# Value products in one group, and a new order of side tiles, turns and vector steps

## The reference

```
x = x + 0.5 * ffn(layernorm(x))      # "1"
x = x +       attn(layernorm(x))     # "2"
x = x + 0.5 * ffn(layernorm(x))      # "3"

ffn(x):  h = relu(x @ W_fc.T)**2;  y = h @ W_proj.T      # 128 -> 512 -> 128
         mem = 0; 5 times: reset = mem > 1; mem = 0.9*mem + y - reset; count += (mem > 1)
         return count / 5
attn(x): q, k, v = split(x @ w_qkv); per head h:
         p = softmax(q k^T / 8 - slope_h * |i - j|, masked above the diagonal)
         return concat(p v) @ w_out + b_out
```

## Time and profile before

| | |
|---|---|
| median of the runs | 1765.89 us |
| profiled execution, span | 1764.1 us |
| TensorE products busy | 1676.8 us, 95% |
| VectorE busy | 1206.1 us, 68% |
| ScalarE busy | 1289.0 us, 73% |
| POOL busy | 920.2 us, 52% |
| 16 DMA engines busy, queue q1 | 42.9% |
| value products (L388) | 2048 instructions, 361.0 us busy |
| transposes of turns (L373) | 2560 instructions, 373.6 us busy |

### The profile page before, as it was taken

One profiled execution on the slowest core, in us unless ns is written; L12 is line 12 of the kernel. 1 busy time (PEld: TensorE's weight loads), 2 busy tenths in 40 slices (PEclk: granted clock), 3 DMA queues, 4 the chain that ended last, 5 costly groups with the idle time before them and its releaser, 6 DMA issues.

```text
span 1764.1 us, 39796 instructions
## 1 busy us (share of the span) xinstructions
PE 1676.8 (95%) x10902; PEld 1259.1 (71%) x10902; DVE 1206.1 (68%) x4272; ACT 1289.0 (73%) x3446; POOL 920.2 (52%) x1258
## 2 busy tenths in 40 slices
PE   4899999999999999999999999999999999999996
PEld 3767777677776777767777676776777677677775
DVE  6575776748777585775858768586785848767563
ACT  2687876777877787876877768687777868868781
POOL 2455554555545455545555545465454545546451
PEclk8999999999999999999999999999999999999998
DMA  2555453435434435443545434444443544434430
GB/s 73 114 109 111 85 119 75 102 82 109 101 81 107 89 84 108 92 104 76 105 93 107 96 82 107 90 87 107 90 103 78 109 95 94 102 82 101 94 82 13
DMA packets 80562, 164.80 MB, mean 93 GB/s; under 512 B 12880, under 2 KB 30928, under 8 KB 80208
## 3 DMA queue, kind: packets, MB, share of 16 engines
q1 hardware_dynamic: 80336, 162.12, 42.9%
HBM read 6.88 MB, written 4.19 MB: 6 GB/s over the span
## 4 chain that ended last, share of the span: by engine, by line
PE 69%; DVE 19%; issue 8%; POOL 2%; ACT 1%; DVEq 1%; DMA 1%; SPq 0%; POOLq 0%; ACTq 0%
PE bank L388 12%; PE bank L373 12%; PE bank L343 7%; PE bank L359 7%; PE bank L431 7%; PE bank L360 6%; PE bank L439 6%; PE bank L345 5%; PE bank L344 5%; DVE spikes L615 3%; DVE negsc L558 3%; DVE negmem L621 2%; DVE drive L618 2%; DVE xn L591 1%; DVE rsum L567 1%
## 5 line engine op out<-in xcount | busy, mean ns | idle before, releaser
L911 POOL TENSOR_TENSOR prob<-prob,rsum 128x512 f32<-128x512 f32 (+3 forms) x1024 | 731.7, 730 | 699.9 <-DVE rsum L567 699.6
L799 ACT ACTIVATE prob<-negsc,negmax 128x512 f32<-128x512 f32 (+3 forms) x1024 | 574.4, 565 | 124.2 <-DVE negmax L558 117.7
L810 ACT COPY probT<-bank 128x512 f32<-128x512 f32 x640 | 362.0, 587 | 194.5 <-PE bank L373 191.9
L558 DVE CUSTOM_DVE_ANT_0 negsc<-bank,alibi 128x512 f32<-128x512 f32 (+3 forms) x1024 | 466.2, 473 | 5.3 <-PE bank L360 5.3
L567 DVE RECIPROCAL rsum<-sums 128x1 f32<-128x1 f32 (+1 forms) x768 | 121.4, 158 | 483.3 <-PE bank L360 466.3
L373 PE MATMUL bank<-ident,prob 128*128 128x128 f32 x2560 | 373.6, 277 | 1.9 <-ACT probT L810 0.2
L359 PE MATMUL bank<-keys,queries 128*128 128x256 f32 (+2 forms) x1024 | 352.1, 355 | 23.1 <-DVE negmax L558 14.4
L388 PE MATMUL bank<-probT,vals 128*64 128x256 f32 (+3 forms) x2048 | 361.0, 453 | 0.3 <-ACT attT L817 0.3
L373 PEld LDWEIGHTS bank<-ident,prob 128*128 128x128 f32 x2560 | 296.2, 141 | 39.4 <-issue 28.6
L360 PE MATMUL bank<-keys,queries 128*128 128x256 f32 (+2 forms) x1024 | 321.2, 325 | 0.0
L359 PEld LDWEIGHTS bank<-keys,queries 128*128 128x128 f32 x1024 | 194.8, 190 | 74.6 <-DVE negmax L558 30.5
(11 more groups left out here) (82 smaller groups left out, 2246.3 us busy)
## 6 DMA issues: line engine op xcount, KB each, us to landing
queries<-queries SPq DMA_DIRECT2D x384, 256.0 KB, 3.0
keys<-k_lo SPq DMA_DIRECT2D x256, 128.0 KB, 2.4
keys<-keys SPq DMA_DIRECT2D x128, 128.0 KB, 3.7
x_in<-in_L_attn_x_dram SPq DMA_DIRECT2D x16, 256.0 KB, 2.9
out_dram<-x SPq DMA_DIRECT2D x16, 256.0 KB, 2.4
prob<-in_L_attn_w_qkv_dram SPq DMA_DIRECT2D x1, 1536.0 KB, 9.1
wo<-in_L_attn_w_out_dram SPq DMA_DIRECT2D x1, 512.0 KB, 10.7
probT<-in_L_ffn_W_fc_dram SPq DMA_DIRECT2D x1, 256.0 KB, 3.2
```

What stands on the lines that cost most here:

```text
L558: ins = dve.tensor_tensor_reduce(negsc[:, k % 3, col:col + WIDTH[i]], src, alibi[:, 2 * p + h, N - WIDTH[i]:N], 1.0, MASKED, ALU.add, ALU.min,
L799: ins = act.activation(prob[:, p % 2, h, PCOL[i]:PCOL[i] + WIDTH[i]], negsc[:, k % 3, col:col + WIDTH[i]], ACT.Exp, bias=negmax[:, p % 2, ...
L810: act.copy(probT[:, turn_slot(p, t), :], turn_bank[(len(TRUNS) * p + t) % 2][:, :]).then_inc(s_turned_out, 1)
L911: ins = pool.tensor_tensor(pr, pr, rsum[:, p % 2, seg:seg + 1].to_broadcast([P, WIDTH[i]]), ALU.mult)
```

## The change

All four value products of a pair run at beat 4 of their slot, j = 0 to 3, where before j = 2 ran at beat 0, j = 1 and 3 at beat 2, and j = 0 at beat 4. Turn 2 goes from beat 3 to beat 4. The order of turns (T), value products (P) and side tiles (D) inside a beat is given by PEORDER for each beat. SIDE holds the same 43 tiles at new places and in a new order, which also says which tile follows which in a bank. SPIKE1, SPIKE3 and the layer norm steps are given beat by beat, at new places. What each instruction computes, and how many there are, stays as it is.

```diff
--- before.py
+++ after.py
@@ -35,9 +35,10 @@
 TRUNS = [[(1, 2), (0, 2)], [(1, 1), (1, 3)], [(0, 1), (0, 3)], [(1, 0)], [(0, 0)]]
 TNEEDS = [max(SEG_TILE[h, i] for h, j in runs for i in range(j, NT)) for runs in TRUNS]
 TRING = 8
-TBEAT = [1, 2, 3, 5, 5]
+TBEAT = [1, 2, 4, 5, 5]
 ATTBEAT = 4
-PV = [[2], [], [1, 3], [], [0], []]
+PV = [[], [], [], [], [0, 1, 2, 3], []]
+PEORDER = ["DPT", "TPD", "TDP", "PTD", "TPD", "PTD"]
 PVORDER = [j for js in PV for j in js]
 
 PVLAST = [max(PVORDER.index(j) for _, j in runs) for runs in TRUNS]
@@ -53,34 +54,26 @@
             col += (NT - jj) * P
 
 
-def beats_from(slot, beat, counts):
-
-    at = [divmod(slot * BEATS + beat + n, BEATS) for n in range(len(counts))]
-    return [x for x, c in zip(at, counts) for _ in range(c)]
-
-
-
-
-
 SIDE = [
-    (0, 0, "q", 0, 0), (0, 1, "k", 0, 0), (0, 3, "v", 0, 0), (0, 4, "t1", 0, 1), (0, 4, "v", 1, 0),
-    (1, 0, "q", 0, 0), (1, 1, "k", 0, 0), (1, 2, "fc1", 0, 1), (1, 4, "fc1", 1, 1), (1, 4, "fc1", 2, 1),
-    (2, 0, "fc1", 3, 1), (2, 0, "q", 0, 0), (2, 1, "out", 0, -1), (2, 1, "out", 1, -1), (2, 2, "y1", 0, 1),
-    (2, 2, "k", 0, 0), (2, 3, "out", 2, -1), (2, 4, "y1", 1, 1), (2, 5, "v", 0, 0),
-    (3, 0, "v", 1, 0), (3, 0, "q", 0, 0), (3, 1, "k", 0, 0), (3, 2, "out", 3, -1),
-    (4, 0, "k", 0, 0), (4, 0, "q", 0, 0), (4, 2, "t3", 0, -1), (4, 3, "v", 0, 0), (4, 4, "v", 1, 0),
-    (5, 0, "q", 0, 0), (5, 1, "fc3", 0, -1), (5, 2, "k", 0, 0), (5, 4, "fc3", 1, -1), (5, 4, "fc3", 2, -1),
-    (5, 5, "fc3", 3, -1),
-    (6, 0, "q", 0, 0), (6, 1, "k", 0, 0), (6, 2, "y3", 0, -1), (6, 2, "y3", 1, -1), (6, 3, "t2", 0, 1),
-    (6, 4, "v", 0, 0), (6, 5, "v", 1, 0),
-    (7, 0, "q", 0, 1), (7, 1, "k", 0, 1),
+    (0, 1, "k", 0, 0), (0, 1, "q", 0, 0), (0, 4, "v", 0, 0), (0, 4, "t1", 0, 1), (0, 5, "v", 1, 0),
+    (1, 0, "fc1", 0, 1), (1, 1, "k", 0, 0), (1, 2, "q", 0, 0), (1, 4, "fc1", 1, 1), (1, 4, "fc1", 2, 1),
+    (1, 5, "out", 0, -1),
+    (2, 0, "out", 1, -1), (2, 0, "fc1", 3, 1), (2, 2, "y1", 0, 1), (2, 3, "q", 0, 0), (2, 3, "k", 0, 0),
+    (2, 4, "y1", 1, 1), (2, 4, "out", 2, -1), (2, 5, "v", 0, 0),
+    (3, 0, "q", 0, 0), (3, 1, "out", 3, -1), (3, 2, "k", 0, 0), (3, 4, "v", 1, 0),
+    (4, 0, "k", 0, 0), (4, 0, "q", 0, 0), (4, 3, "t3", 0, -1), (4, 4, "v", 0, 0), (4, 4, "fc3", 0, -1),
+    (4, 5, "v", 1, 0),
+    (5, 0, "q", 0, 0), (5, 1, "k", 0, 0), (5, 3, "fc3", 1, -1), (5, 4, "fc3", 2, -1), (5, 4, "fc3", 3, -1),
+    (6, 0, "k", 0, 0), (6, 1, "y3", 0, -1), (6, 1, "y3", 1, -1), (6, 1, "q", 0, 0), (6, 3, "t2", 0, 1),
+    (6, 5, "v", 0, 0),
+    (7, 0, "v", 1, 0), (7, 1, "q", 0, 1), (7, 2, "k", 0, 1),
 ]
 
-SPIKE1 = beats_from(3, 0, [2, 3, 1, 1, 0, 0, 1, 1, 1, 1, 2, 1])
-SPIKE3 = beats_from(6, 3, [1, 2, 2, 1, 2, 1, 2, 1, 2])
-LN1 = dict(stats=(0, 0), aggregate=(0, 1), rstd=(0, 1), normalise=(0, 3))
-LN2 = dict(stats=(5, 2), aggregate=(5, 3), rstd=(5, 3), normalise=(6, 1))
-LN3 = dict(stats=(3, 4), aggregate=(3, 5), rstd=(3, 5), normalise=(4, 0))
+SPIKE1 = [(2, 5), (2, 5), (3, 0), (3, 1), (3, 4), (3, 4), (4, 4), (4, 4), (4, 4), (4, 4), (5, 0), (5, 3), (5, 4), (5, 4)]
+SPIKE3 = [(6, 3), (6, 3), (6, 3), (6, 5), (6, 5), (7, 0), (7, 1), (7, 1), (7, 2), (7, 3), (7, 3), (7, 5), (7, 5), (7, 5)]
+LN1 = dict(stats=(0, 1), aggregate=(0, 2), rstd=(0, 3), normalise=(0, 3))
+LN2 = dict(stats=(5, 4), aggregate=(6, 0), rstd=(6, 1), normalise=(6, 1))
+LN3 = dict(stats=(3, 2), aggregate=(3, 3), rstd=(3, 4), normalise=(3, 4))
 
 
 def macaron_kernel(nc: bass.Bass, x, w_qkv, w_out, b_out, w_fc, w_proj, out):
@@ -477,14 +470,17 @@
                 for k in range(BEATS):
                     if exists(b, s):
                         scores(b, s, k, par)
-                    for j in PV[k]:
-                        if exists(*pv_of):
-                            pv(*pv_of, j)
-                    for t in range(len(TRUNS)):
-                        if TBEAT[t] == k and exists(*t_of):
-                            turn(*t_of, t)
-                    for n, kind, i, off, _ in side_at(s, k, offsets):
-                        side(n, kind, i, off, b, s, par, last_user(n, b, offsets))
+                    for part in PEORDER[k]:
+                        if part == "P" and exists(*pv_of):
+                            for j in PV[k]:
+                                pv(*pv_of, j)
+                        elif part == "T":
+                            for t in range(len(TRUNS)):
+                                if TBEAT[t] == k and exists(*t_of):
+                                    turn(*t_of, t)
+                        elif part == "D":
+                            for n, kind, i, off, _ in side_at(s, k, offsets):
+                                side(n, kind, i, off, b, s, par, last_user(n, b, offsets))
                     if between:
                         between(k)
```

## The result

The changed kernel takes 1725.9 us (1722.93 to 1729.04, four runs) against 1766.25: ratio 0.977 [0.9754, 0.9787], 40 us less. The forecast was 82 us less. The profiled execution has a span of 1725.5 us (1764.1 before). TensorE's lines stand 7 lower than before (scores L352, turns L366, value products L381, transposes of x L408), SP's in `place` too, VectorE's 4 lower.

The account below looks back on a forecast made before the run. The prediction took TensorE to bound slots 1 to 6 and VectorE slots 7 to 0. Its terms, 3.9 + 0.7 + 0.54 = 5.1 us a batch, took 82 us off 1764.1, giving a 1684 us median, range 1662 to 1706.

Parts of the forecast that it names:

- The group, 0.65 us a pair: TensorE's value products: one group for three saves 0.65 us a pair in group, entry and exit costs, 83 us over 128 pairs.
- the entry: TensorE's swap from turn 2's transposes into the value group: taken as 0.08 us, though the trace had no such pair.
- The lower end, a free swap: Transposes into the value group cost nothing extra at entry, in place of 0.08 us; moves the sum by 10 us.
- the upper: Transposes into the value group cost twice the entry, 0.16 us, making the TensorE gain 73 us.
- Slots 1 to 6, 5.1 us a batch: TensorE-bound slots shorten: 3.9 us from grouping, 0.7 from moved v tiles, 0.54 in slot 4; 82 us over 16 batches.
- slot 4's wait for t3's bank: In slot 4, v waits for VectorE to read t3 from their shared bank; all 0.54 us a batch taken as gone.
- Slots 7 and 0, nothing: VectorE is full there, so TensorE's shorter stream only waits longer for the normalised x; gain counted as nothing.
- The late keys of slot 7: Slot 0's scores start up to 1.7 us later, covered by 2.1 us before t1; price 0, or 27 us uncovered.
- The step that failed: Later q and k tiles in the slots other than 7 cost nothing, those slots having more room for the copies.
- VectorE binds in five slots: Rival: slots 3 and 5 become VectorE-bound too, leaving gain in slots 1, 2 and 6: 42 us, 1724 us; chance 0.10.
- the swap does not get cheaper: Rival: transposes ahead of the group or four j's order cost what fewer swaps save: gain 42 us, 1724 us; chance 0.05.
- the slower rival, late keys: Rival: late keys idle TensorE at slot ends and drop its clock, 5.1 us each; two a batch give 1848 us; chance 0.08.

Follow-up runs that it names:

- the loop written out: Loop over batches unrolled on TensorE, VectorE, ScalarE and POOL: kernel before 1743.74 us, changed kernel 1692.65 us, changed kernel with the keys first 1674.52 us.
- the keys first: Changed kernel with SP issuing the two key copies ahead of the two query copies in slots 0, 4 and 6: 1700.67 us, ratio 0.9629.
- the slot 7 experiment: Kernel with the keys first, slot 7's q moved to beat 0, k to beat 1, its v tile back to slot 6: 1719.01 us, ratio 0.9725.
- early q and k: Changed kernel with q and k tiles a beat or more earlier in slots 0, 1, 6 and 7: 1762.89 us, ratio 0.9981.
- the group alone: Kernel before with only the value products grouped at beat 4, turn 2 and beat order as changed: 1780.55 us; with turn 2 and order as before: 1772.97 us.

## Why the prediction was wrong

*The group, 0.65 us a pair:* right, 0.62, and so is the choice of 0.08 for the entry that the trace did not show (0.09). The lower end, a free swap, was wrong; so was the upper, for which the prediction read the Trainium skill, TensorEngine Tiling (Restrictions): a transpose ahead of the group costs no more than a score product does.

*Slots 1 to 6, 5.1 us a batch:* 3.7 measured, 4.4 between the two kernels with the loop written out, 4.7 with the keys first, 5.0 with both (82.0 to 77.0). So the sum was right but for what the step below left out and what the loop costs. The parts are right in kind: slots 2, 3 and 5 have no gap of note, and slot 4's wait for t3's bank is gone.

*Slots 7 and 0, nothing:* right where no loop end stands (22.8 and 23.1; 22.7 and 22.8 with the loop written out), 0.9 us short at loop ends. The late keys of slot 7 cost next to nothing, as the step had it: the wait at the start of slot 0 grew from 0.23 us at 878.77 to 1.73 at 866.40, and the wait for t1, 1.43 in the earlier trace rows, is gone. That the wait for t1 is the cover is not shown: where the slot 7 experiment takes the wait for keys away, waits for POOL and ScalarE come in its place and not that one.

*The step that failed* is the price of the late q and k outside slot 7, put at nothing: "In the other slots q and k also come up to a beat later, but a slot of 11 to 17 us leaves more room than slot 7." It took 3.7 us from k's low half as the whole way. Where k stands ahead of q, SP stands at q's low half and needs 5.9 us from there, and the new tables put k first in slots 0, 1 and 6, beside slot 4, where it was first before. So the scores waited at the ends of slots 6 and 0 and within slot 1; the order of four copies alone is worth 25 us.

*Not in the sum at all:* the first batch, counted like any other (5.1 us less), takes 8.1 more. Slot 1 alone takes 4.6 more (9.3 to 13.9). Its first slots have no turns, value products or tiles of a batch before to cover the copies, which is the likely reason; early q and k take 5.3 of it back, the rest is not settled. Nor is the loop's end in the sum, whose cost the forecast left as it is: it read the 2.53 us that slot 7 lacks as room, and they are the wait behind a branch (last section).

Worked out by batches: 14 x (5.1 - 3.7) = 20 in slots 1 to 6, 14 x 0.6 = 8 in slots 7 and 0, 13 in the first batch: 41 of the 43 us between 82 and the 38.6 of the two spans. Keys and loop ends are causes inside the first two sums and are not added to them. With the keys first and the loop written out the kernels are 69 us apart (1743.7 to 1674.5), and the first batch is most of what is then left to 82.

*The rivals:* the time lies where "VectorE binds in five slots" and "the swap does not get cheaper" had put it (1724), and that is a coincidence, as both are wrong: in slots 3 and 5 TensorE has no gap (11.08 of 11.08 and 10.67 of 10.67 us) and VectorE works 10.23 and 9.70, and the swap is cheaper. The mechanism that was right is that of the slower rival, late keys, at a third of its size: 25 us for 82, in waits of 0.4 to 2 us, mostly without the slower clock. That stands behind loop ends as before, where TensorE had been idle for 3.27 us (0.88 in the last stretch above, a mean of the levels of 1.2 and 2.4 GHz).

## What to carry to other kernels

Work that an engine does between two instructions is also the time in which others finish for the second: before work is joined into one group, list every bank, copy and tile that used its time as cover, since the group alone cost 15 us here, or 6 with turn 2 left in its place, and paid only with a new order around it. Price a chain of copies from the instruction at which its queue really stands, not from the last thing it needs, and look at the order in which one queue waits for several producers; that was the cheapest 25 us in this kernel. Count the first and last turns of a pipeline apart, where the cover is not there yet.

## What the runs showed of the hardware that was not expected

The branch at the end of this loop holds TensorE's sequencer for 3.5 to 4.4 us in the kernels before and after, of which only the products already queued are hidden. Before the change, at 985.91 in the earlier trace rows, it runs from 981.53 to 985.47; the copies that the next scores wait for had landed by 983.26 and the queued products ended at 983.38, so the 2.53 us that slot 7 lacks there are the branch's. With slot 7 early fewer products are queued and up to 5.66 us are idle. What the branch waits for is not shown. The records of the same branch on the other engines are short:

```profile
L250 POOLq COMPARE_BRANCH  x7: 40/45/45, 345.7 to 1583.7; - x7
L250 ACTq COMPARE_BRANCH  x7: 40/45/45, 346.1 to 1584.1; - x7
L250 DVEq COMPARE_BRANCH  x7: 55/63/63, 348.0 to 1586.0; - x7
```

They are not all of the cost on VectorE. At the end of slot 7 after the change (970.20) its first step behind the branch starts 1.3 us after the scores that it reads have ended:

```profile
970.53 0.40 PE L353 MATMUL bank<-keys,queries 128*128 128x512 f32 x1
972.23 0.17 DVE L563 RECIPROCAL rsum<-sums 128x2 f32<-128x2 f32 x1 [2.52 <-PE bank L353]
```

At the first one VectorE's branch ends at 348.08 and the next instruction of its queue starts at 350.94; on POOL and ScalarE the next comes within 0.4 us.

The one loop exit among TensorE's seven branches takes 83 ns. The Trainium skill, Advanced Engine Details and Errata (Control Flow Timing), gives some 108 ns for a compare-and-branch: that is near the exit and far from the six branches back. An estimate by this figure alone, seven times 108 ns, is under 1 us for writing out the loop; it gained 22, 33 and 26, with the operations on registers gone as well.
